# A gated cross-attention layer: PV and denominators in three bursts per 16 slots instead of four

## The chip, the cores and the metric

The kernel runs on one core of one Trainium2 chip. The metric is the time of one execution on the device in microseconds (us), the median of three runs. Profiles are of one execution each, and all times in them are counted from its first instruction.

## What is computed

Cross-attention with a tanh gate, and behind it a linear layer (called FFN in the code) with a gate of its own. Batch 8, 512 channels in 16 heads of 32, 1024 targets and 1024 sources, float32.

```python
q = einsum('oc,bct->bot', Wq, layernorm(x)) + bq      # k, v alike from ctx
dot = einsum('bhdt,bhds->bhts', q, k) / sqrt(32)
dot = mask * dot - (1.0 - mask) * 1e6
amap = softmax(dot, axis=-1) * mask
x = x + tanh(g_xattn) * einsum('bhts,bhds->bhdt', amap, v)
d1 = fp8(layernorm(x) * scale) / scale                # d2 alike from W2
x = x + tanh(g_ffn) * (d1 @ d2)
```

## The kernel before

A first part, up to some 580 us, projects q, k and v batch by batch and leaves them in DRAM. The second part is the attention. It works on **quads**: four heads of one batch, so 32 quads, `n` from 0 to 31. Each quad is a period of `NSLOT` = 64 **slots** `k`; two further periods drain the pipeline. All engines run through the same slots in program order and meet at semaphores, with no scheduler: what stands in which slot is written out by hand in the functions `slot` and `period` of each engine.

In a slot TensorE does two matmuls of 128x512: `scores` (line 833), whose result is keys by queries for the softmax of quad n, and `scores_for_max` (line 848), the same products the other way round, some of quad n and, from slot 19 (`XLEAD`) on, of quad n+1, from which VectorE takes the row maxima (`maximum`, line 1034, a reduction of 128x512). ScalarE takes the exponential of a score tile (`exp`, line 733) into `probs`, a ring of four chunks of four slots. The score tiles rotate through three PSUM banks, `s_bank`; the maxima tiles through three others, `x_bank`, in which `F_JOBS` also places four extra tenants: the turned maxima (`max1`, `max0`) and the FFN's two halves. So matmul k waits for what was done with the tile three places back:

```python
if counted(NSLOT * n + k - NB3 + 1):
    pe.wait_ge(exp_done, NSLOT * n + k - NB3 + 1)
```

Every four slots a chunk `c` of exponentials is complete. `times_v` (PV, line 863) multiplies it with V: four matmuls, one per head, each on 32 columns of the array, so they run side by side. Every eight slots GpSimd adds the two chunks of a **pair** `r` (`add_pair`, line 478, four additions of 128x512), and `denominators` (line 874) sums it over the keys with four such matmuls on `ones`. I call a set of four matmuls a group, and what stands between two slots' matmuls a burst. Chunk c must be consumed before chunk c+4 is written, pair r before pair r+2; exponentials of pair r+2's first slot wait for all of pair r's additions.

After 32 slots one half (`th`) of the queries is done. ScalarE copies output and denominators out (`copy_o`, `copy_den`), SyncE moves the denominators to 16 values a partition (`move_den`), VectorE inverts them (`invert`, lines 1059 and 1062), SyncE stores them to `inv_scr` (`move_inv`, line 594) and loads them spread over the heads' channels as `inv_b` (`spread_inv`, line 600). GpSimd's `weigh` (line 487) multiplies the copied output with `inv_b`, and `add_residual` (line 493) adds x. Then come the second layernorm and the rounding to fp8, in 15 numbered steps: VectorE's in the tables `NORM_AT` and `NORM_AT_2` (2 and 3 are `bn_stats`, line 1070), ScalarE's in `scale_rstd` and `normalize`, GpSimd's `pow`; then a DMA transpose, the FFN two quads later (`ffn`, line 889, eight matmuls for each half in two slots), `add_ffn` (line 1086) and the store. The next maxima go VectorE's `negate_max`, TensorE's `turn_max` (line 881), ScalarE's `copy_max`, SyncE's `set_max` (line 618) into two rows of `q_st`, which `scores` need from slots 0 and 32 on.

SyncE's issues stand in the fixed order of its `period`; each waits for its own data, and so holds up those behind it. `load_tm` (line 608) waits for the landing of the `inv_b` spread just ahead of it.

## Time and profile before

| | |
|---|---|
| median of three runs | 2563.50 us (2563.49 to 2564.08) |
| the profiled execution | 2563.17 us, of which 2561.4 from its first instruction to its last |
| TensorE, matmuls | 2481.3 us busy, 97% |
| VectorE | 1981.2 us, 77% |
| GpSimd | 1655.9 us, 65% |
| ScalarE | 1391.6 us, 54% |
| granted TensorE clock, mean | 0.990 |
| the attention loop | from some 580 us to the end |

A row of the table by stage has, for each stretch, the busy time of PE, PEld, DVE, ACT and POOL in this order. PE is TensorE, PEld its weight loads, DVE VectorE, ACT ScalarE, POOL GpSimd, SP SyncE (SPq its issues). A line such as "x4" in a timeline stands for four instructions of a kind merged into one row, with the time from the first one's start to the last one's end. A burst of four float32 matmuls shows eight records.

### The profile page before, as it was taken

To read this page: it belongs to the slowest core of one execution; us is meant where nothing else is said; L and a number is where in the kernel's file an instruction comes from. 1 tells how busy PE (TensorE), PEld (TensorE's weight loads), DVE (VectorE), ACT (ScalarE), POOL (GpSimd) and SP (SyncE) were. 2 spreads that over 40 slices of the span, in tenths; PEclk is the share of its full clock that TensorE was granted. 3 is DMA by queue.
4 is the path that set the end of the run, shared out by engine and by line. 5 is a ranking of instruction groups with operands and counts; after the bars stand their busy time and mean duration, and the time that the engine had idled before them with its cause. 6 is when DMAs were issued, how large, how long until landed. Compare 5 with 4: busy or idle time off the path is not lost.

```text
span 2561.4 us, 40583 instructions
## 1 busy us (share of the span) xinstructions
PE 2481.3 (97%) x13169; PEld 1380.6 (54%) x13169; DVE 1981.2 (77%) x3250; ACT 1391.6 (54%) x2606; POOL 1655.9 (65%) x1265
## 2 busy tenths in 40 slices
PE   5999999999999999999999999999999999999995
PEld 4888888874444444444444444444444444444441
DVE  5766666687788888888888888888888888888862
ACT  2333333315666666666666666666666666666562
POOL 1333333426777777777777777777777777777774
PEclk8999999999999999999999999999999999999997
DMA  6666666663444444444443444444444444444411
GB/s 208 239 237 238 239 237 238 238 195 94 95 98 101 102 97 95 90 94 96 92 90 90 90 90 95 93 93 96 100 101 98 101 101 94 93 94 91 97 31 50
DMA packets 242040, 314.49 MB, mean 123 GB/s; under 512 B 75032, under 2 KB 142680, under 8 KB 241856
## 3 DMA queue, kind: packets, MB, share of 16 engines
q1 hardware_dynamic: 229712, 274.20, 42.4%
q10 hardware_dynamic: 12144, 38.02, 4.2%
q8 instruction: 93, 1.52, 0.3%
q14 instruction: 91, 0.75, 0.1%
HBM read 200.09 MB, written 102.11 MB: 118 GB/s over the span
## 4 chain that ended last, share of the span: by engine, by line
PE 86%; DVE 6%; issue 3%; DMA 1%; POOL 1%; ACT 0%; SPq 0%; DVEq 0%; POOLq 0%; ACTq 0%
PE bank L818 20%; PE bank L833 19%; PE bank L863 18%; PE bank L848 16%; PE bank L874 8%; PE bank L889 5%; DVE part_max L1034 4%; POOL pair_sum L478 1%; PE bank L881 1%; DVE y L102 1%; DMA q_st<-qx_scr 0%; DVE isnan L101 0%; DMA v_scr<-stage 0%; POOL y L487 0%; DVE row_max L1043 0%
## 5 line engine op out<-in xcount | busy, mean ns | idle before, releaser
L478 POOL TENSOR_TENSOR pair_sum<-probs 128x512 f32<-128x512 f32 x1024 | 1284.9, 1287 | 425.2 <-ACT probs L733 425.2
L1034 DVE TENSOR_REDUCE part_max<-bank 128x1 f32<-128x512 f32 x2048 | 1282.1, 682 | 336.5 <-PE bank L848 329.1
L733 ACT ACTIVATE probs<-bank 128x512 f32<-128x512 f32 x2048 | 1071.1, 603 | 651.6 <-PE bank L833 648.0
L833 PE MATMUL bank<-q_st,k_st 100*128 100x512 f32 x2048 | 875.3, 429 | 5.1 <-ACT probs L733 5.0
L848 PE MATMUL bank<-k_st,q_st 98*128 98x512 f32 x2048 | 813.1, 397 | 7.6 <-DVE part_max L1034 5.5
L833 PEld LDWEIGHTS bank<-q_st,k_st 100*128 100x128 f32 x2048 | 386.5, 189 | 512.3 <-issue 264.9
L863 PE MATMUL bank<-probs,v_t 128*32 128x512 f32 x4096 | 546.3, 605 | 0.0
L848 PEld LDWEIGHTS bank<-k_st,q_st 98*128 98x128 f32 x2048 | 388.1, 190 | 112.9 <-DVE part_max L1034 9.9
L469 POOL TENSOR_TENSOR stage_lo<-stage,stage_hi 128x512 fp32r<-128x512 f32 x128 | 188.9, 1498 | 133.9 <-ACT stage_hi L697 133.0
L874 PE MATMUL bank<-pair_sum,ones 128*32 128x512 f32 x2048 | 267.4, 594 | 2.8 <-POOL pair_sum L478 2.8
L697 ACT ACTIVATE stage_hi<-stage 128x512 fp32r<-128x512 f32 x128 | 79.8, 632 | 200.6 <-DVE stage L948 140.0
L863 PEld LDWEIGHTS bank<-probs,v_t 128*32 128x32 f32 x4096 | 80.6, 108 | 144.0 <-ACT probs L733 75.5
L889 PE MATMUL bank<-w2q,y_t 128*128 128x512 bf16 x512 | 135.2, 390 | 23.1 <-DMA y_t<-y 22.7
L874 PEld LDWEIGHTS bank<-pair_sum,ones 128*32 128x32 f32 x2048 | 66.5, 110 | 156.3 <-issue 152.0
L457 POOL TENSOR_TENSOR rstd<-ve,neg_half 128x4 f32<-128x4 f32 x8 | 14.7, 1832 | 209.8 <-DVE ve L979 209.8
L818 PE MATMUL bank<-c_hi,w_hi_k 128*128 128x512 f32 x256 | 100.5, 393 | 13.8 <-DVE c_lo L931 13.8
L714 ACT ACTIVATE stage<-stage,sm_now 128x512 f32<-128x512 f32 x64 | 44.6, 720 | 120.9 <-DVE stage L944 120.9
L818 PE MATMUL bank<-w_hi_v,c_hi 128*128 128x512 f32 x256 | 100.2, 391 | 0.0
L818 PE MATMUL bank<-w_hi_v,c_lo 128*128 128x512 f32 x256 | 100.1, 391 | 0.0
L818 PE MATMUL bank<-c_hi,w_lo_k 128*128 128x512 f32 x256 | 100.1, 391 | 0.0
L818 PE MATMUL bank<-w_lo_v,c_hi 128*128 128x512 f32 x256 | 100.1, 391 | 0.0
L818 PE MATMUL bank<-c_lo,w_hi_k 128*128 128x512 f32 x256 | 100.1, 391 | 0.0
(95 smaller groups left out, 1966.0 us busy)
## 6 DMA issues: line engine op xcount, KB each, us to landing
k_st<-k_scr SPq DMA_DIRECT2D x96, 512.0 KB
q_st<-q_scr SPq DMA_DIRECT2D x192, 256.0 KB
c_raw<-in_ctx_dram ACTq DMA_DIRECT2D x32, 512.0 KB, 7.0
x_raw<-in_x_dram ACTq DMA_DIRECT2D x32, 512.0 KB, 6.3
k_scr<-stage_hi SPq DMA_DIRECT2D x64, 256.0 KB, 2.5
k_scr<-stage_lo SPq DMA_DIRECT2D x64, 256.0 KB, 2.7
v_scr<-stage SPq DMA_DIRECT2D x64, 256.0 KB, 2.9
q_scr<-stage_hi SPq DMA_DIRECT2D x64, 256.0 KB, 2.1
```

Of the source, the lines that this page charges most:

```text
L469: nc.gpsimd.tensor_tensor(stage_lo[:, e % STG], stage[:, g % STG], stage_hi[:, e % STG].bitcast(F32), ALU.subtract).then_inc(qk_lo, 1)
L478: nc.gpsimd.tensor_tensor(pair_sum[:, r % 2, h], probs[:, a, h], probs[:, a + 1, h], ALU.add).then_inc(pair_done, 1)
L697: nc.scalar.activation(stage_hi[:, e % STG], stage[:, g % STG], ACT.Copy).then_inc(qk_hi, 1)
L714: nc.scalar.activation(stage[:, g % STG], stage[:, g % STG], ACT.Copy, scale=sm_now[:, j:j + 1]).then_inc(v_masked, 1)
L733: nc.scalar.activation(probs[:, c % PR, h, :], s_bank_of(n, k)[:, :], ACT.Exp).then_inc(exp_done, 1)
L818: last = nc.tensor.matmul(acc, a, m, start=(cb == 0 and n == 0), stop=(cb == CB - 1 and n == 2))
L833: nc.tensor.matmul(s_bank_of(n, k)[:, :], k_st[p][0:KS, h, j * P:(j + 1) * P], q_st[p][0:KS, th, h, :], start=True, stop=True).then_inc(sc ...
L848: nc.tensor.matmul(x_bank_of(n, "tile", k)[:, :], q_st[p][0:KX, th, h, tc * P:(tc + 1) * P], k_st[p][0:KX, h, sh * HALF:(sh + 1) * HALF], ...
L863: last = nc.tensor.matmul(o_bank[D * h:D * (h + 1), :], v_t[p][:, j, D * h:D * (h + 1)], probs[:, c % PR, h, :], start=(j == 0), stop=(j = ...
L874: last = nc.tensor.matmul(d_bank[D * h:D * (h + 1), :], ones[:, :], pair_sum[:, r % 2, h, :], start=(i == 0), stop=(i == 3))
L889: last = nc.tensor.matmul(x_bank_of(n, f"ffn{half}", k)[:, :], y8_t[:, kc, :], w2q[:, kc, half * HALF:(half + 1) * HALF], start=(kc == 0), ...
L1034: nc.vector.tensor_reduce(part_max[:, th, sh, at:at + 1], x_bank_of(n, "tile", k)[:, :], AX, ALU.max).then_inc(max_done, 2)
```

## The change

The groups keep their number and shapes and get other slots. Written for 16 slots `16i` to `16i+15`: before, a burst stood behind slots 3, 7, 11 and 15, one PV group in each, and one denominator group more in those behind 3 and 11. After, bursts of two groups stand behind slots 5, 10 and 15: denominators and PV, denominators and PV, PV and PV. The side work on the other engines gets other slots, and `weigh` with `add_residual` stand behind GpSimd's pair 2 instead of pair 3.

```diff
-            F_JOBS = {23: "max1", 34: "ffn0", 50: "ffn1", 55: "max0"}
+            F_JOBS = {22: "max1", 40: "ffn0", 56: "ffn1", 54: "max0"}
@@ GpSimd, period
-                            if r == 3 and real(n - 1):
+                            if r == 2 and real(n - 1):
                                 weigh(n - 1)
                                 add_residual(n - 1, 1 - p)
@@ ScalarE, period
-                            if k == 3 and real(n - 1):
+                            if k == 5 and real(n - 1):
                                 copy_o(n - 1, 1)
-                            if k == 23 and real(n):
-                                copy_max(n, n, 1, 23)
-                            if k == 35 and real(n):
+                            if k == 22 and real(n):
+                                copy_max(n, n, 1, 22)
+                            if k == 37 and real(n):
                                 copy_o(n, 0)
-                            if k == 44 and real(n):
+                            if k == 45 and real(n):
                                 copy_den(n, 0)
-                            if k == 50 and real(n - 1):
+                            if k == 55 and real(n - 1):
                                 scale_rstd(n - 1)
-                            if k == 51 and real(n - 1):
+                            if k == 55 and real(n - 1):
                                 normalize(n - 1, 1 - p)
-                            if k == 55 and real(n + 1):
-                                copy_max(n, n + 1, 0, 55)
+                            if k == 54 and real(n + 1):
+                                copy_max(n, n + 1, 0, 54)
@@ TensorE, slot
-                        if k == 23 and real(n):
+                        if k == 22 and real(n):
                             turn_max(n, k, n, 1)
-                        if k == 55 and real(n + 1):
+                        if k == 54 and real(n + 1):
                             turn_max(n, k, n + 1, 0)
-                        for half, at_ in ((0, 34), (1, 50)):
+                        for half, at_ in ((0, 40), (1, 56)):
-                        if k % 4 == 3:
-                            if k >= 7 and real(n):
-                                times_v(n, p, (k - 7) // 4)
-                            if k < 7 and real(n - 1):
+                        i, at_ = k // 16, k % 16
+                        if at_ == 5:
+                            if i > 0 and real(n):
+                                denominators(n, 2 * i - 2)
+                                times_v(n, p, 4 * i - 1)
+                            if i == 0 and real(n - 1):
+                                denominators(n - 1, 6)
                                 times_v(n - 1, 1 - p, 15)
-                        if k % 8 == 3:
-                            if k >= 19 and real(n):
-                                denominators(n, (k - 19) // 8)
-                            if k < 19 and real(n - 1):
-                                denominators(n - 1, 6 + k // 8)
+                        if at_ == 10:
+                            if i > 0 and real(n):
+                                denominators(n, 2 * i - 1)
+                            if i == 0 and real(n - 1):
+                                denominators(n - 1, 7)
+                            if real(n):
+                                times_v(n, p, 4 * i)
+                        if at_ == 15 and real(n):
+                            times_v(n, p, 4 * i + 1)
+                            times_v(n, p, 4 * i + 2)
@@ VectorE, slot
-                    NORM_AT = {43: (2, 3), 44: (4,), 45: (5,), 59: (9, 10)}
-                    NORM_AT_2 = {3: (11,), 11: (12,), 19: (13, 14)}
+                    NORM_AT = {39: (2, 3,), 40: (4,), 44: (5,), 58: (9,), 61: (10,)}
+                    NORM_AT_2 = {3: (11,), 7: (12,), 14: (13,), 19: (14,)}
-                        if k == 19 and real(n):
+                        if k == 20 and real(n):
                             negate_max(n, 1)
-                        if k == 35 and real(n - 2):
-                            add_ffn(n, n - 2, p, 0, 34)
-                        if k == 51 and real(n - 2):
-                            add_ffn(n, n - 2, p, 1, 50)
+                        if k == 41 and real(n - 2):
+                            add_ffn(n, n - 2, p, 0, 40)
+                        if k == 58 and real(n - 2):
+                            add_ffn(n, n - 2, p, 1, 56)
-                        if k == 55 and real(n):
+                        if k == 54 and real(n):
                             invert(n, 0)
```

`invert(n - 1, 1)` stays at slot 23, `negate_max(n + 1, 0)` at 51, `copy_den(n - 1, 1)` at 12. SyncE's order of issues is the same. The line numbers after the change are 10 higher from VectorE's part on.

TensorE where the first half of the FFN stands, before: slot 34, the first four of its matmuls, slot 35, the other four, and the burst right behind them.

```order
L833 MATMUL bank<-q_st,k_st 128x512
L848 MATMUL bank<-k_st,q_st 128x512
L889 MATMUL bank<-w2q,y_t 128x512 x4
L833 MATMUL bank<-q_st,k_st 128x512
L848 MATMUL bank<-k_st,q_st 128x512
L889 MATMUL bank<-w2q,y_t 128x512 x4
L863 MATMUL bank<-probs,v_t 32x512 x4
L874 MATMUL bank<-pair_sum,ones 32x512 x4
```

The same place of the changed kernel, slots 40 to 42 and the burst behind 42.

```order
L889 MATMUL bank<-w2q,y_t 128x512 x4
L833 MATMUL bank<-q_st,k_st 128x512
L848 MATMUL bank<-k_st,q_st 128x512
L889 MATMUL bank<-w2q,y_t 128x512 x4
L833 MATMUL bank<-q_st,k_st 128x512
L848 MATMUL bank<-k_st,q_st 128x512
L874 MATMUL bank<-pair_sum,ones 32x512 x4
L863 MATMUL bank<-probs,v_t 32x512 x4
```

The second part of the half now has a slot behind it, and the burst begins with the denominators, here those of pair 3.

GpSimd, one quad of the middle, before: pair additions (28 from pair 5 of one quad to pair 3 of the next), the two long steps, pair 4, and the `pow`.

```order
L478 TENSOR_TENSOR pair_sum<-probs 128x512 x28
L487 TENSOR_TENSOR y<-o_raw,inv_b 128x1024
L493 TENSOR_TENSOR res<-res,y 128x1024
L478 TENSOR_TENSOR pair_sum<-probs 128x512 x4
L504 TENSOR_TENSOR rs<-ve,neg_half 128x1
```

And in the changed kernel:

```order
L478 TENSOR_TENSOR pair_sum<-probs 128x512 x24
L487 TENSOR_TENSOR y<-o_raw,inv_b 128x1024
L493 TENSOR_TENSOR res<-res,y 128x1024
L478 TENSOR_TENSOR pair_sum<-probs 128x512 x8
L504 TENSOR_TENSOR rs<-ve,neg_half 128x1
```

The four additions of pair 3 moved from in front of the two long steps to behind them.

VectorE in the changed kernel, from the inversion of the previous quad (slot 23) to slot 44: the reductions are those of the maxima tiles.

```order
L1069 RECIPROCAL inv_c<-den_c 128x16
L1072 SCALAR_TENSOR_TENSOR inv_c<-inv_c,g,tm_c 128x16
L1044 TENSOR_REDUCE part_max<-bank 128x1 x16
L1080 BN_STATS st<-res 128x6 x2
L1044 TENSOR_REDUCE part_max<-bank 128x1
L1082 BN_AGGR mv<-st 128x2
L1044 TENSOR_REDUCE part_max<-bank 128x1
L1096 SCALAR_TENSOR_TENSOR res<-bank,g,res 128x512
L1044 TENSOR_REDUCE part_max<-bank 128x1 x3
L1086 TENSOR_SCALAR ve<-mv 128x1
```

The two `bn_stats` now stand behind the tile of slot 39, the second of a run; before, they stood behind that of slot 43, the last ahead of a burst.

## Rows read from the trace of the kernel before

**Rows 1.** The page's span; one stretch: its length, busy us of five engines, clock, DMA, GB/s

```profile
span 2561.4 us, 40583 instructions
...
1500.00:2000.00 500.00, 497.38 (x2785) 240.51 (x2784) 411.21 (x711) 308.33 (x602) 372.29 (x288) 1.00 0.43 96
```

**Rows 2.** The list of waits of the whole run: total us, times, longest us

```profile
ACT o_raw L739 <- POOL y L487: 69.1, 31, 3.4
...
PE bank L848 <- DVE part_max L1034: 5.5, 5, 4.2
```

**Rows 3.** TensorE's timeline, 1500.9 to 1506.5: start us, us, engine, line, names

```profile
1500.87 0.39 PE L848 MATMUL bank<-k_st,q_st 98*128 98x512 f32 x1
...
1502.53 0.40 PE L848 MATMUL bank<-k_st,q_st 98*128 98x512 f32 x1
...
1503.94 0.40 PE L848 MATMUL bank<-k_st,q_st 98*128 98x512 f32 x1
...
1506.47 0.40 PE L848 MATMUL bank<-k_st,q_st 98*128 98x512 f32 x1
```

**Rows 4.** Timeline of all engines in the fourth slot of two runs

```profile
1496.04 1.29 DVE L1034 TENSOR_REDUCE part_max<-bank 128x1 f32<-128x512 f32 x2 [0.58 <-PE bank L848]
...
1496.79 0.19 PEld L848 LDWEIGHTS bank<-k_st,q_st 98*128 98x128 f32 x1
1496.94 0.40 PE L848 MATMUL bank<-k_st,q_st 98*128 98x512 f32 x1
...
1503.84 0.19 PEld L848 LDWEIGHTS bank<-k_st,q_st 98*128 98x128 f32 x1 [0.18 <-issue]
```

**Rows 5.** Timelines of VectorE and of ScalarE, 1502.8 to 1530.2

```profile
1503.03 2.48 DVE L1034 TENSOR_REDUCE part_max<-bank 128x1 f32<-128x512 f32 x4 [0.58 <-PE bank L848]
...
1507.00 2.48 DVE L1034 TENSOR_REDUCE part_max<-bank 128x1 f32<-128x512 f32 x4
...
1509.67 0.37 DVE L1062 SCALAR_TENSOR_TENSOR inv_c<-inv_c,g,tm_c 128x16 f32<-128x16 f32 x1
...
1528.78 1.41 DVE L1070 BATCH_NORM_STATS2 st<-res 128x6 f32<-128x512 f32 x2
...
1502.81 2.07 ACT L733 ACTIVATE probs<-bank 128x512 f32<-128x512 f32 x4 [0.51 <-PE bank L833]
```

**Rows 6.** TensorE's timeline around a turn and the FFN's two halves

```profile
1508.42 0.30 PE L881 MATMUL bank<-ident_r,neg_max 128*128 128x128 f32 x1
...
1517.91 0.39 PE L848 MATMUL bank<-k_st,q_st 98*128 98x512 f32 x1
...
1519.41 0.39 PE L848 MATMUL bank<-k_st,q_st 98*128 98x512 f32 x1
...
1520.61 1.06 PE L863 MATMUL bank<-probs,v_t 128*32 128x512 f32 x8
```

**Rows 7.** SyncE's timeline, 1510.4 to 1517.6

```profile
1510.46 0.71 SPq L618 DMA_DIRECT2D q_st<-max_rows  x1
1511.50 0.55 SPq L600 DMA_DIRECT2D inv_b<-inv_scr  x1
1516.50 1.06 SPq L608 DMA_DIRECT2D tm_c<-tm_scr  x2
```

**Rows 8.** GpSimd's timeline, 1519.9 to 1529.7

```profile
1519.88 2.37 POOL L487 TENSOR_TENSOR y<-o_raw,inv_b 128x1024 f32<-128x1024 f32 x1
...
1524.68 5.01 POOL L478 TENSOR_TENSOR pair_sum<-probs 128x512 f32<-128x512 f32 x4
```

**Rows 9.** DMA issues by line: KB each, median us to landing

```profile
out_dram<-res SPq DMA_DIRECT2D x32, 512.0 KB, 2.6
...
inv_scr<-inv_c SPq DMA_DIRECT2D x64, 8.0 KB, 1.4
```

**Rows 10.** SyncE's timeline in another quad, 1147.3 to 1153.0

```profile
1147.26 0.54 SPq L600 DMA_DIRECT2D inv_b<-inv_scr  x1
1151.91 1.06 SPq L608 DMA_DIRECT2D tm_c<-tm_scr  x2
```

More of the change, by code:

```diff
@@ L722, in batch @@
                             if not more and g == G - 4:
-                                copy_max(-1, 0, 0, 55)
+                                copy_max(-1, 0, 0, 54)
                     def exp(n, k):
```

## The prediction

> **What bounds the kernel now.** I read the page's span first, 2561.4 us, and then the table by stage: in a stretch of the attention loop TensorE is busy 497.38 of 500 us, at the full clock [rows 1]. So in that loop a microsecond taken from TensorE's stream shortens the run unless another engine takes its place. The list of waits says how near the others are: over the whole run TensorE waited 5.5 us for VectorE's row maxima, and ScalarE, not TensorE, waited 69.1 us for GpSimd's `y` [rows 2]. Then I read TensorE's timeline over one burst of each kind, and timelines of the other four engines for the slack.
>
> I write m(k) for the start of slot k's second matmul (the maxima one, line 848). Two slots apart without anything between them it is 0.467 us per slot (1503.94 less 1502.53 is 1.41 for three).
>
> **The saving in bursts.** A burst of one group takes m(k+1) to 1.66 us after m(k) (1500.87 to 1502.53), a burst of two groups to 2.53 us (1503.94 to 1506.47) [rows 3]. Less the plain slot that is 1.19 and 2.06 us. Before, 16 slots hold two of each, 6.50 us; after, three of two groups, 6.18 us. The work is the same six groups of four matmuls, and one entry and exit of about 0.32 us is gone. Per quad (64 slots) 4 x 0.32 = 1.28 us are saved. Groups in another order (denominators first, or two PV groups) have no row; between 1.74 us (no entry at all) and 2.38 us (two whole single bursts) I take 2.06, as the weight loads and columns are the same.
>
> **First loss: VectorE's lag with longer runs of slots.** A slot's maxima tile goes into one of three banks, so m(k+3) waits until the reduction of tile k has ended. The reduction starts 0.50 us after its matmul (1503.03 against 1502.53); four of them take 2.48 us, one 0.68, so the next starts every 0.60 us, slower than the 0.467 us of a slot [rows 3, 5]. In the fourth slot of a run the weight load already comes late: it starts at 1496.79, 0.07 us after the first reduction's end (1496.04 + 0.68), instead of with the matmul before it; its own matmul at 1496.94 still is on time, and in another run one started 0.10 us after such a load (1503.84, 1503.94) [rows 3, 4]. So m(i+3) cannot come before 0.50 + 0.60 i + 0.68 + 0.06 + 0.10 = 1.34 + 0.60 i us after the run's first. Runs of four slots: 1.34 against 1.40, no stall, as the trace has it. After, the runs are 6, 5 and 5 slots. Fifth slot: 1.94 against 1.87, a stall of 0.07. Sixth: 2.54 against 1.94 + 0.47, another 0.13, so 0.20 in a run of six. Per quad four runs of six lose 0.80. Of the eight runs of five, those with a `turn_max` (slots 22 and 54) lose nothing, since the turn spaces the slots out; five plain ones lose 0.35. In slots 38 to 42 the two halves of the FFN make the room (their slots take 1.50 and 1.20 + 0.13 us [rows 6]: natural length 3.77 us), but two `bn_stats`, 1.41 us, now stand after tile 39, and slot 42 needs tile 40: reduction from 3.03 us, end 3.71, m(42) at 3.87: 0.10 lost. Sum 1.25 us. VectorE's other steps stand behind the third tile of a run or further, or behind a tile that only the next run needs; the burst of 2.06 us covers them, as it does for the longest (1.2 us), with about 0.2 us to spare. Without that cover each costs what it sticks out. ScalarE's exponentials come every 0.49 us (2.07 less 0.60, over three) [rows 5], only 0.02 slower than a slot, and never gate six.
>
> **Second loss: GpSimd's two long steps ahead of pair 3.** `weigh` and `add_residual` move from behind the fourth pair addition to behind the third. `weigh` waits for `inv_b`, whose chain starts with `invert` behind tile 23 and is not moved. From m(23): 0.50 + 0.68 for the reduction, then 0.56 until the inversion's end (1509.67 + 0.37 less 1509.48), so 1.74 us. From there the way through two DMAs to the landing is 6.46 us: 1510.04 to 1516.50, where SyncE's next issue had waited for it [rows 5, 7]. Its longest part, from the issue of the second DMA to that point, is 5.00 us here and 4.65 us in the quad at 1147 [rows 7, 10], so 6.1 to 6.5 us in all. `weigh` and `add_residual` take 4.80 us (1519.88 to 1524.68), the four additions of pair 3 then 5.01 us [rows 8], handovers 0.10. So pair 3 is summed 1.74 + 6.46 + 4.80 + 5.01 + 0.10 = 18.11 us after m(23). TensorE wants it at slot 42, first thing in the burst (`denominators(n, 3)`). Its own way there: three slots 1.40, burst 2.53, slots 27 to 31 1.94, burst 2.53, slots 32 to 37 2.53, burst 2.53, slots 38 to 42 3.87, and 0.24 to the weight load: 17.57. It waits 0.54 us. Behind it stand that burst and every later slot. Before, pair 3 was added as soon as its exponentials were there and `weigh` began 3.4 us after the landing; that cover is spent. Exponential 40 also waits for pair 3, but its bank is wanted only after the burst.
>
> The Trainium skill (page "DMA: Bandwidth & Descriptors", section "Anatomy of one DMA — SWDGE (gpsimd) path") gives about 2.0 us plus bytes over 436 GB/s for one DMA, and so 2.6 us, an estimate, for the 256 KB of `inv_b`. The trace has 5.00 us from its issue to the next instruction that waits for it (1511.50 to 1516.50) [rows 7]. By the page the wait at slot 42 would vanish and the sum would end at 2564.
>
> **The other edits.** `turn_max` at slots 22 and 54: the transposed maxima are ready well over a microsecond earlier, behind a burst. FFN halves at 40 and 56, ScalarE's copies and normalize: each has a burst or two slots of slack; the price is nothing, up to 0.1 us per quad either way, since a turn or an FFN half now meets a slot instead of a burst. If `normalize` had no burst behind it, its 1.2 us would stop slot 59.
>
> **Sum.** Per quad -1.28 + 1.25 + 0.54 = +0.51 us. Thirty quads (1 to 30) have both losses: +15.3. Quad 0 has no `weigh`: 0. In the last quad the slots are shorter, so the wait for pair 3 is longer while the maxima losses end at slot 18, and in the tail `add_ffn` comes in front of one step of the last chain: about +1.5 together. The profiled execution took 2563.2 us (2561.4 between its first and last instruction), 0.3 below the median of the runs. 2563.5 + 16.8 is 2580.
>
> **The rivals.**
> - Pair 3 is in time (the way to slot 42 longer, or `inv_b` sooner, by over 0.54 us; a store of 512 KB lands in 2.6 us [rows 9]). Then the burst saving and VectorE's lag cancel: -1.28 + 1.25, 2564, no change. Against it: even the shorter 6.1 us leave 0.2 us of wait.
> - VectorE's lag doesn't stall (the weight load may begin before the reduction ends, or matmuls need less than 0.10 us behind it). TensorE then reaches slot 42 0.37 us earlier and waits 0.91: -1.28 + 0.91, 30 times, and 1.5: 2554, faster. For it: no such stall has a row in this trace. Against it: the weight load is seen held back to the reduction's end in the fourth slot. It decides once the five- and six-slot stalls are under half of what I say.
> - Neither loss comes: -1.28 x 31, 2524, faster. This is the change doing what bursts alone promise.
> - SyncE's queue. `store` now waits for the second `add_ffn` behind slot 58 instead of 51, and `set_max(n+1, 0)` stands behind it; slot 0 of the next quad needs that. The add ends 1.85 us after m(58); `store` and `move_inv` are issued first, at most 0.71 us each, so `set_max` is issued at 3.3 at most and lands 1.4 to 2.6 us later [rows 7, 9], by 5.9, against slot 0 at 2.53 + 1.94 + 2.19 = 6.66. Should it land like `inv_b`, after 5.0 us, slot 0 waits 1.6 us in every quad: 2628.
>
> **How the numbers follow.** Chances: as forecast 0.68; pair 3 in time 0.13; VectorE without stall 0.08; neither 0.05; SyncE's queue or another wait of that size 0.06. The likeliest gives 2580, its own range 2568 to 2592 (0.4 us per quad either way: the landing varies by 0.35, and a third of the VectorE stalls is as much). The whole range, taking in the case of no change and most of the faster one down to 2556, ends at 2596 above. Under 0.2%, 5.1 us, a measurement of this kernel can't tell a difference. Slower: 0.68 + 0.06 = 0.74, less a little for a forecast that shrinks, 0.72; within 0.2%: 0.15; faster 0.13.
>
> **What would show it.** In the profile after: m to m over every burst 2.53 us; in runs of five and six slots the fifth and sixth distance between line-848 matmuls over 0.467 by 0.07 and 0.13, with PEld's waits on `part_max` in the list; at the burst behind slot 42 a wait of about 0.5 us for `pair_sum` in every quad, with `y` (line 487) starting right at `inv_b`'s landing, some 8.6 us after the start of the turn (line 881) instead of 11.5 [rows 6, 8]; ScalarE's longest wait moves from `o_raw` to exponential 40. The forecast is wrong if line 874 never waits for `pair_sum`, if the burst costs more than 2.1 us, or if scores of slot 0 wait for `max_rows`.

## The result and the profile after

The changed kernel takes 2783.6 us, the median of four runs (2780.1 to 2789.4), against 2563.8 us for the kernel before on the same chip: ratio 1.086 (95% interval 1.084 to 1.087), 220 us more. The forecast had the direction and missed the size by far: 2580 us, range 2556 to 2596.

The page of the changed kernel: span, section 1, and the start of section 4, the chain that ended last.

```profile
span 2784.9 us, 40583 instructions
...
PE 2576.4 (93%) x13169; PEld 1392.7 (50%) x13169; DVE 2061.1 (74%) x3250; ACT 1391.5 (50%) x2606; POOL 1702.1 (61%) x1265
...
PE 56%; DMA 24%; POOL 5%; SPq 5%; DVE 4%; issue 4%; ACT 1%; DVEq 0%; POOLq 0%; ACTq 0%
PE bank L818 18%; DMA q_st<-qx_scr 18%; PE bank L848 11%; PE bank L833 10%; PE bank L863 8%; PE bank L874 6%; POOL pair_sum L478 4%; DMA inv_scr<-inv_c 3%; DMA inv_b<-inv_scr 3%; PE bank L889 2%; DVE part_max L1044 2%; SPq L570 2%; SPq L577 2%; POOL y L487 1%; DVE res L1096 1%
```

TensorE is busy 95 us longer with the same instructions, so it ran slower for a part of the time; the rest of the 223 us of span is idle. And 18% of the chain is a DMA that no step of the prediction named: `q_st<-qx_scr`, the last of those loads of the next quad's K and Q for which slot 19 waits.

The list of waits of the changed kernel (total us, times, longest us):

```profile
POOL pair_sum L478 <- PE bank L874: 282.6, 95, 8.7
...
PEld bank L848 <- DVE part_max L1044: 198.7, 602, 5.0
...
POOL y L487 <- DMA inv_b<-inv_scr: 191.2, 32, 13.5
...
ACT probs L733 <- POOL pair_sum L478: 98.7, 31, 4.9
PE bank L848 <- DMA q_st<-qx_scr: 97.1, 29, 4.5
...
PE bank L874 <- POOL pair_sum L478: 17.3, 18, 3.3
```

The waits for `part_max` and at L874, and `y` starting on the landing of `inv_b`, were forecast. The fifth line was not, and is the largest wait of TensorE's matmuls. None of the prediction's three signs of being wrong shows: L874 does wait, a double burst costs no more than 2.1 us, and no `scores` wait for `max_rows`. Where it comes from is on SyncE. First its timeline in the changed kernel at the end of a quad, then the same place before the change:

```profile
1453.36 0.36 SPq L627 DMA_DIRECT2D out_dram<-res  x1
1453.76 0.43 SPq L594 DMA_DIRECT2D inv_scr<-inv_c  x1
1454.23 0.74 SPq L618 DMA_DIRECT2D q_st<-max_rows  x1
1456.22 0.55 SPq L600 DMA_DIRECT2D inv_b<-inv_scr  x1
1456.87 1.37 SPq L570 DMA_DIRECT2D k_st<-k_scr  x3
...
1462.18 0.29 SPq L579 DMA_DIRECT2D q_st<-qx_scr  x1
```

```profile
1538.45 0.36 SPq L627 DMA_DIRECT2D out_dram<-res  x1
1542.29 0.34 SPq L594 DMA_DIRECT2D inv_scr<-inv_c  x1
...
1543.72 0.55 SPq L600 DMA_DIRECT2D inv_b<-inv_scr  x1
1547.74 1.29 SPq L570 DMA_DIRECT2D k_st<-k_scr  x3
```

Before, the store went out 4 us ahead of `inv_scr`, and the 256 KB of `inv_b` 4.0 us ahead of the K and Q loads. After, the store waits for `add_ffn` behind slot 58, everything behind it goes out in one lump, and `inv_b` is 0.65 us ahead of the loads. TensorE's timeline at slot 19, whose maxima matmul is the first to use the new K and Q:

```profile
1474.22 0.39 PE L833 MATMUL bank<-q_st,k_st 100*128 100x512 f32 x1
1478.82 0.80 PE L848 MATMUL bank<-k_st,q_st 98*128 98x512 f32 x1 [4.21 <-DMA q_st<-qx_scr]
1479.41 0.63 PE L833 MATMUL bank<-q_st,k_st 100*128 100x512 f32 x1
```

It stands 4.2 us, and the matmuls behind it take 0.63 us where those of [rows 3] take 0.40. The table by stage, around this wait (columns as in [rows 1]):

```profile
1458.10:1474.20 16.10, 16.10 (x90) 7.96 (x87) 14.88 (x22) 10.11 (x20) 13.42 (x11) 1.00 1.01 193
1474.20:1478.90 4.70, 0.49 (x3) 0.08 (x1) 1.24 (x3) 1.20 (x3) 0.61 (x1) 0.88 0.77 147
1478.90:1486.00 7.10, 7.10 (x27) 2.99 (x27) 3.36 (x8) 1.94 (x5) 2.58 (x3) 0.60 0.31 70
1486.00:1526.80 40.80, 40.15 (x226) 18.69 (x224) 32.42 (x57) 24.16 (x48) 30.21 (x23) 1.00 0.11 35
```

While the loads run (first row) the DMA engines are full, 1.01; the kernel before has 0.99 there (1548 to 1564 us). After the wait the granted clock is 0.60 over 7.1 us, most of that time at the lower level of 1.2 GHz, and then full again.

Where each quad's time goes I worked out from all records of `scores` in quads 4 to 29: mean us from one slot's `scores` to the next one's, the burst behind the slot included, and of that the time at 1.2 GHz. The columns e1, e5 and e8 are experiments further down, and "best" is the last one, e11.

```
slots                    after   e1      e5      e8      best
32 to 37 (run of six)    5.07    5.07    5.06    5.07    5.07
6 to 10 (run of five)    4.47    4.46    4.47    4.47    4.47
11 to 15                 5.04    5.05    5.05    5.03    5.03
19                       4.24    0.47    0.47    0.48    0.48
20, 21 (burst)           4.78    3.08    3.08    3.07    3.08
22 (turn)                0.90    3.34    0.63    0.63    0.63
23 to 26 (burst)         4.31    6.20    4.40    4.40    4.40
42 (burst, pair 3)       3.29    2.76    3.82    2.79    2.79
57                       2.09    2.15    2.02    2.18    1.34
all 64                  68.15   66.56   62.98   62.10   61.26
of that at 1.2 GHz       5.78    4.99    0.13    0       0
```

The kernel before takes 60.74 us for the same 64 slots, none of it at 1.2 GHz; there a slot with a double burst is 2.42, one with a single burst 1.55, the slot behind either 0.57 and a plain one 0.47. "after" less "best" is 6.89 us a quad: slots 19 to 26 5.6, slot 42 0.5, slot 57 0.75.

The forecast stalls themselves are there. TensorE's timeline at the end of a run of six slots, and at the burst behind slot 42:

```profile
1628.24 0.40 PE L848 MATMUL bank<-k_st,q_st 98*128 98x512 f32 x1
...
1628.71 0.48 PE L848 MATMUL bank<-k_st,q_st 98*128 98x512 f32 x1
...
1629.29 0.50 PE L848 MATMUL bank<-k_st,q_st 98*128 98x512 f32 x1
...
1636.78 1.07 PE L874 MATMUL bank<-pair_sum,ones 128*32 128x512 f32 x8 [0.61 <-POOL pair_sum L478]
```

### The profile page after: what moved, and what is told of

Its sections match the earlier page's. It is cut to its first block, busy times and chain, and to the rows that moved or that the text cites. A ratio compares the mean times of both kernels' runs of the same rounds, so it can differ in the third digit from the quotient of the medians.

```text
span 2784.9 us, 40583 instructions
## 1 busy us (share of the span) xinstructions
PE 2576.4 (93%) x13169; PEld 1392.7 (50%) x13169; DVE 2061.1 (74%) x3250; ACT 1391.5 (50%) x2606; POOL 1702.1 (61%) x1265
## 4 chain that ended last, share of the span: by engine, by line
PE 56%; DMA 24%; POOL 5%; SPq 5%; DVE 4%; issue 4%; ACT 1%; DVEq 0%; POOLq 0%; ACTq 0%
PE bank L818 18%; DMA q_st<-qx_scr 18%; PE bank L848 11%; PE bank L833 10%; PE bank L863 8%; PE bank L874 6%; POOL pair_sum L478 4%; DMA inv_scr<-inv_c 3%; DMA inv_b<-inv_scr 3%; PE bank L889 2%; DVE part_max L1044 2%; SPq L570 2%; SPq L577 2%; POOL y L487 1%; DVE res L1096 1%
## 5 line engine op out<-in xcount | busy, mean ns | idle before, releaser
L1044 DVE TENSOR_REDUCE part_max<-bank 128x1 f32<-128x512 f32 x2048 | 1298.9, 682 | 490.8 <-PE bank L848 488.4
L478 POOL TENSOR_TENSOR pair_sum<-probs 128x512 f32<-128x512 f32 x1024 | 1330.6, 1333 | 481.8 <-PE bank L874 282.6
L733 ACT ACTIVATE probs<-bank 128x512 f32<-128x512 f32 x2048 | 1085.5, 606 | 851.6 <-PE bank L833 744.9
L848 PE MATMUL bank<-k_st,q_st 98*128 98x512 f32 x2048 | 890.5, 435 | 122.0 <-DMA q_st<-qx_scr 97.1
L833 PE MATMUL bank<-q_st,k_st 100*128 100x512 f32 x2048 | 890.0, 436 | 2.1 <-ACT probs L733 1.9
L848 PEld LDWEIGHTS bank<-k_st,q_st 98*128 98x128 f32 x2048 | 397.3, 194 | 372.3 <-DVE part_max L1044 198.7
L863 PE MATMUL bank<-probs,v_t 128*32 128x512 f32 x4096 | 531.3, 614 | 0.0
L874 PE MATMUL bank<-pair_sum,ones 128*32 128x512 f32 x2048 | 298.0, 656 | 17.6 <-POOL pair_sum L478 17.3
L863 PEld LDWEIGHTS bank<-probs,v_t 128*32 128x32 f32 x4096 | 123.8, 113 | 280.4 <-issue 222.1
L487 POOL TENSOR_TENSOR y<-o_raw,inv_b 128x1024 f32<-128x1024 f32 x32 | 76.5, 2390 | 191.2 <-DMA inv_b<-inv_scr 191.2
```

The source lines that it names most:

```text
L478: nc.gpsimd.tensor_tensor(pair_sum[:, r % 2, h], probs[:, a, h], probs[:, a + 1, h], ALU.add).then_inc(pair_done, 1)
L487: nc.gpsimd.tensor_tensor(y[:, :], o_raw[:, :, :].rearrange("p a t -> p (a t)"), inv_b[:, :, :].rearrange("p a t -> p (a t)"), ALU.mult).t ...
L733: nc.scalar.activation(probs[:, c % PR, h, :], s_bank_of(n, k)[:, :], ACT.Exp).then_inc(exp_done, 1)
L833: nc.tensor.matmul(s_bank_of(n, k)[:, :], k_st[p][0:KS, h, j * P:(j + 1) * P], q_st[p][0:KS, th, h, :], start=True, stop=True).then_inc(sc ...
L848: nc.tensor.matmul(x_bank_of(n, "tile", k)[:, :], q_st[p][0:KX, th, h, tc * P:(tc + 1) * P], k_st[p][0:KX, h, sh * HALF:(sh + 1) * HALF], ...
L863: last = nc.tensor.matmul(o_bank[D * h:D * (h + 1), :], v_t[p][:, j, D * h:D * (h + 1)], probs[:, c % PR, h, :], start=(j == 0), stop=(j = ...
```

## The experiments

### Round 1: the queue, the burst table alone

**e1_store_last.** The changed kernel with SyncE's store moved behind the spread. Theory: the late store makes slot 19 wait. Rival: VectorE's side steps in the longer runs.

```diff
-                        if real(n - 2):
-                            store(n - 2, p)
                         if real(n):
                             move_inv(n, 0)
                         if real(n + 1):
                             set_max(n + 1, 0, 1 - p)
                         if real(n):
                             spread_inv(n, 0)
+                        if real(n - 2):
+                            store(n - 2, p)
```

> The changed kernel with one edit: SyncE issues the store of quad n-2 behind the spread of inv_b for (n, 0), at the end of its period, instead of in front of move_inv(n, 0). Theory Q (the queue): in the changed kernel that store waits for the FFN's second add behind slot 58, so the inv_b spread (256 KB, about 3.5 us of packets) is issued 1.9 us ahead of slot 0, right in front of the next quad's K and Q loads, and these land about 4 us later than slot 19 wants them; TensorE's idle time there also brings the granted clock to half for some 7 us. Then with this edit the spread is issued at least 4 us ahead of slot 0 again, the wait at slot 19 (now 3.6 us in the mean) is under 0.3 us, no stretch at half clock is left in the loop, and a quad takes 61 to 62 us: 2575 to 2600 us. Rival S (the slots): K and Q are late because of the new order of TensorE's bursts and the longer steps on VectorE and GpSimd; then the wait stays over 2 us and the time over 2720. Rival C (the clock gate alone, tripped by the waits at slot 42 and at the turns): the wait at slot 19 goes, but stretches at half clock stay, 2620 to 2700.

Measured: 2740.9 us, 1.069 (1.067 to 1.070). The wait at slot 19 is gone (0.47 in the table), which refutes the rival, and yet only 43 us came back, where 2575 to 2600 us were expected: behind slot 22 TensorE now waits for `neg_max` in nearly every quad. The timeline of all engines there, the list of waits, and the table by stage around it:

```profile
1591.69 3.72 POOL L478 TENSOR_TENSOR pair_sum<-probs 128x512 f32<-128x512 f32 x3 [2.29 <-PE bank L874]
1591.74 1.26 DVE L1053 TENSOR_TENSOR row_max<-part_max 128x16 f32<-128x16 f32 x1
...
1593.04 1.18 DVE L1058 TENSOR_SCALAR neg_max<-row_max 128x16 fp32r<-128x16 f32 x1
1594.26 1.19 DVE L1060 SCALAR_TENSOR_TENSOR neg_max<-row_max,neg_max 128x16 fp32r<-128x16 f32 x1
...
1595.50 0.47 PE L881 MATMUL bank<-ident_r,neg_max 128*128 128x128 f32 x1 [2.40 <-DVE neg_max L1060]
```

```profile
PE bank L881 <- DVE neg_max L1060: 69.5, 29, 2.4
```

```profile
1590.40:1595.50 5.10, 2.70 (x19) 0.72 (x19) 5.03 (x7) 1.17 (x3) 3.72 (x3) 0.98 0.31 65
1595.50:1600.50 5.00, 5.00 (x17) 3.08 (x21) 4.39 (x8) 2.66 (x5) 1.27 (x1) 0.50 0.02 3
```

Three steps on 16 columns take 1.2 us each. Where nothing meets them each takes 0.16 to 0.18 us, the shortest of the run; the median of the two `neg_max` steps is that too, 0.18 us, while `row_max` has a median of 0.87, as nearly all of them start beside an addition. They run beside three GpSimd additions of 1.24 us that begin at 1591.69, and each ends with one: 1593.00, 1594.22, 1595.45 against 1592.93, 1594.17, 1595.41. Behind the wait of 2.4 us the clock is 0.50, that is 1.2 GHz, for 5 us.

**e2_late_spread.** The kernel before, with SyncE held ahead of `spread_inv(n, 0)` until slot 62, so that `inv_b` goes out 0.9 us ahead of the loads. Nothing else is touched.

```diff
                         if real(n):
+                            sp.wait_ge(scores_ready, NSLOT * n + 62)
                             spread_inv(n, 0)
```

> The kernel before with one wait more: SyncE issues the inv_b spread of (n, 0) only when the scores of slot 61 are done, some 2 us ahead of slot 0, as in the changed kernel, instead of 5.1 us ahead. Nothing else differs; the value is not wanted before slot 28 of the next quad. Theory Q: K and Q land some 4 us later, a wait of 3 to 4 us at slot 19 appears in every quad with half clock behind it, a quad takes 66 to 68 us, 2700 to 2780 us in all. Rival S: no wait at slot 19, within 0.3% of 2564. A weaker form of Q (the spread matters only together with the store of 512 KB, which is issued 5 us ahead of slot 0 in the changed kernel): a wait of 1 to 2 us, 2600 to 2650.

Measured: 2662.6 us, 1.039 (1.032 to 1.045). The list of waits:

```profile
PE bank L849 <- DMA q_st<-qx_scr: 65.7, 28, 4.6
```

Slot 19 takes 5.93 us instead of 2.42, 2.9 us per quad fall at the lower clock, the quad takes 64.42 us instead of 60.74. The first K load goes out 1.1 us ahead of slot 0, exactly as in the kernel before, so the loads do not start later; they land later. The place of `inv_b` in the queue alone makes the wait in a kernel that had none. At 2663 us the loss is smaller than theory Q had it (2700 to 2780).

**e3_bursts_alone.** The kernel before with only the new burst table (the TensorE part of the diff from `i, at_ = k // 16, k % 16` on) and ScalarE's copies at 5, 37 and 45, where the groups end; turn, FFN, VectorE, GpSimd and SyncE as before.

```diff
-                            if k == 3 and real(n - 1):
+                            if k == 5 and real(n - 1):
                                 copy_o(n - 1, 1)
-                            if k == 35 and real(n):
+                            if k == 37 and real(n):
                                 copy_o(n, 0)
-                            if k == 44 and real(n):
+                            if k == 45 and real(n):
                                 copy_den(n, 0)
```

> The kernel before with TensorE's new bursts (three of two groups per 16 slots) and ScalarE's copies of outputs and denominators behind the groups they need (slots 5, 37, 45); turns, FFN, weigh, norm steps and invert stay where they were. By the sum of the prediction: bursts -1.28 us per quad; VectorE's lag +0.07 in the fifth and +0.13 in the sixth slot of a run, but turns and FFN halves (slots 23, 34, 50, 55) now stand inside runs and give room, so +0.8 to +1.1; pair 3 is not moved, no wait at slot 42. So -0.2 to -0.5 us per quad and 2548 to 2560 us, if no wait for K and Q appears at slot 19. Rival: VectorE's side work at slots 11, 35, 43, 51, which now stands early in a run, stalls TensorE by more than the bursts save: 2565 to 2600.

Measured: 2767.3 us, 1.080 (1.078 to 1.082). Here the side steps stand early in a run and no burst covers them: slots 15, 47 and 53 take 3.1 to 3.8 us, slot 63 5.85. The timeline of three engines at slot 63:

```profile
1644.05 1.65 DVE L94 TENSOR_SCALAR big<-big 128x1024 f32<-128x1024 f32 x1
...
1645.61 2.47 DVE L1042 TENSOR_REDUCE part_max<-bank 128x1 f32<-128x512 f32 x4
...
1646.35 0.49 PE L848 MATMUL bank<-k_st,q_st 98*128 98x512 f32 x1 [2.09 <-DVE part_max L1042]
```

The burst behind it runs partly at the lower clock. The rival was right about the side steps and, with 2565 to 2600 us, far too low about their price. So the new places of the side work are not the fault of the change as such: without them the new bursts cost nearly as much by another way.

**e4_store_last_weigh3.** e1 with `weigh` and `add_residual` back behind pair 3 (`r == 3`). 

> e1 and one edit more: weigh and add_residual stand behind GpSimd's pair 3 again. By the prediction's second loss pair 3 then is in time for slot 42: 0.5 us per quad less than e1, so 12 to 20 us faster than e1, with no wait for pair_sum at the burst behind slot 42. Rival: bn_stats at slot 39 now waits for the residual, holds up the maxima tile of slot 40 and gives the gain back: within 5 us of e1.

Measured: 2748.7 us, 1.072 (1.071 to 1.074), nothing gained over e1, where 12 to 20 us were expected. In e1 the wait for `pair_sum` at L874 is 6.5 us in the whole run: the 2.4 us at the turn had given GpSimd the time. The forecast wait can't be seen as long as a longer one stands ahead of it.

### Round 2: GpSimd beside VectorE

**e5_negate_early.** e1 with `negate_max(n, 1)` behind tile 19, ahead of the additions, and step 14 in its place.

```diff
-                    NORM_AT_2 = {3: (11,), 7: (12,), 14: (13,), 19: (14,)}
+                    NORM_AT_2 = {3: (11,), 7: (12,), 14: (13,), 20: (14,)}
-                        if k == 20 and real(n):
+                        if k == 19 and real(n):
                             negate_max(n, 1)
```

> e1 (the changed kernel with the store last in SyncE's period) and one edit more: VectorE's negate_max stands behind the tile of slot 19, as before the change, and norm step 14 behind slot 20. In e1 the turn behind slot 22 waits 2.5 us a quad for neg_max: negate_max, three short steps behind slot 20, falls together with GpSimd's pair 2, which starts as soon as the denominators behind slot 21 are done, and each step takes about 1.2 us instead of 0.17. Theory P (VectorE's steps on SBUF wait for GpSimd's running addition): at slot 19 GpSimd is idle, the three steps take 0.17 us each again, the turn's wait and the half-clock stretch behind it go: 4 to 5 us a quad less than e1, 61.5 to 63 us, 2590 to 2630 us. Rival C (the clock falls for another reason, such as the form of the new bursts): the wait goes but some 5 us a quad at half clock stay: 2660 to 2700.

Measured: 2636.6 us, 1.027 (1.025 to 1.029), 7 us above the range of theory P. Slot 22 falls from 3.34 to 0.63 us, the time at the lower clock from 5.0 to 0.1 us per quad. Now the wait for pair 3 is out in the open: slot 42 takes 3.82 us, and the list of waits has

```profile
PE bank L874 <- POOL pair_sum L478: 34.6, 31, 3.3
```

**e6_half_additions.** e1 with each pair addition on 256 of its 512 columns, 1.0 standing in the other half. It leaves out the sum for half the columns. Theory: VectorE's long steps wait for the running addition, so shorter additions shorten them.

```diff
-                            nc.gpsimd.tensor_tensor(pair_sum[:, r % 2, h], probs[:, a, h], probs[:, a + 1, h],
-                                                    ALU.add).then_inc(pair_done, 1)
+                            nc.gpsimd.tensor_tensor(pair_sum[:, r % 2, h, 0:HALF // 2], probs[:, a, h, 0:HALF // 2],
+                                                    probs[:, a + 1, h, 0:HALF // 2], ALU.add).then_inc(pair_done, 1)
```

> e1 with GpSimd's pair additions on 256 of 512 columns; it leaves out the sum over the other half of the columns, which holds ones, so the denominators there are wrong and the rest is unchanged. An addition then takes about 0.65 us instead of 1.25. Theory P: a VectorE step that meets GpSimd waits for at most the addition under way, so neg_max's two steps fall from 1.19 to about 0.6 us, y (L98) from 2.13 to about 1.5, isnan from 0.94 to 0.6 or less, the wait at the turn from 2.5 to about 0.7, and with it the half clock goes: 2600 to 2650. Rival D (these steps are long because the DMA traffic of K and Q slows VectorE's SBUF access, or by their own place): their durations stay at 1.1 us and over, and the time stays within 1% of e1.

Measured: 2579.0 us, 1.005 (1.003 to 1.007), faster than the 2600 to 2650 of theory P. The view of one tile, `neg_max`, in e1 and then in e6 (min/median/max in ns):

```profile
L1060 DVE SCALAR_TENSOR_TENSOR neg_max<-row_max,neg_max x56: 174/177/1186, 630.1 to 2460.9; 128x16 fp32r<-128x16 f32 x56
```

```profile
L1060 DVE TENSOR_SCALAR neg_max<-row_max x61: 174/176/679, 628.9 to 2464.8; 128x16 fp32r<-128x16 f32 x61
```

(The two edits shift the line numbers against each other, so L1060 is the second step there and the first here; both steps read 174 to 177 where nothing meets them.) The longest goes from 1.19 to 0.68 us as the addition's median goes from 1.28 to 0.73 us, and `y<-y,big` (line 98) from 2.13 to 1.77. How long these two wait is thus set by the addition's length. One step does not follow: `isnan` has a median of 0.94 in e1 and, in e6,

```profile
L101 DVE TENSOR_SCALAR isnan<-y x29: 411/982/998, 714.3 to 2429.2; 128x1024 bf16<-128x1024 bf16 x29
```

where 0.6 or less was expected; why it stays long no run shows. Slots 11 to 15 go from 5.05 to 4.68, slot 22 from 3.34 to 1.20, slot 57 to 1.34, and no time is left at 1.2 GHz.

**e7_before_negate21.** The kernel before with `negate_max(n, 1)` at slot 21 instead of 19. 

> The kernel before with one edit: negate_max for th = 1 stands behind the tile of slot 21 instead of 19; the turn stays behind slot 23. In the trace of before GpSimd's pair 2 begins at about slot 21. Theory P: the three steps of negate_max now meet those additions, take about 1.2 us each, the turn waits some 2 us in every quad, and the granted clock drops behind that wait as in e1: 2 to 4 us a quad, 2620 to 2690 us. Rival (the length of these steps comes from something else in the new order): they stay at 0.17 us, no wait, 2560 to 2570.

Measured: 2728.8 us, 1.066 (1.062 to 1.069), 65.64 us per quad, more than the 2620 to 2690 us expected: two slots' delay of three short steps costs 165 us. The list of waits:

```profile
PE bank L881 <- DVE neg_max L1050: 94.2, 31, 3.3
```

Slot 23 takes 5.44 us instead of 2.01, and 4.6 us per quad pass at the lower clock.

### Round 3: how much comes back

**e8_weigh3.** e5 with `r == 3`. 

> e5 and one edit more: weigh and add_residual behind GpSimd's pair 3 again, as before the change. In e5 TensorE waits 1.4 us a quad for pair 3 at the burst behind slot 42, the second loss of the prediction, larger than its 0.54. If that loss is what the move of the two steps costs, slot 42 takes 2.4 to 2.5 us instead of 3.8 and a quad 61.5 to 61.8: 2595 to 2605 us. Rival: pair 4 or the bn_stats of slot 39, which need the residual, become late instead, and the time stays over 2620.

Measured: 2612.6 us, 1.019 (1.017 to 1.020), above the 2595 to 2605 expected. Slot 42 goes from 3.82 to 2.79 us, not to 2.4 to 2.5: with nothing else in the way the order on GpSimd costs 1.03 us a quad.

**e9_invert56.** e8 with `invert(n, 0)` behind tile 56 instead of 54. 

> e8 and one edit more: invert(n, 0) behind the tile of slot 56 instead of 54. In e5 slot 57 takes 2.0 us against 1.34 with shorter GpSimd additions (e6), since the second step of invert meets GpSimd in the first slot of a run and tile 55 comes late. Two slots on, only the next run wants the tiles behind it: 0.6 us a quad less than e8, 2575 to 2590 us. Rival: the inversion now comes too late for SyncE, the spread of inv_b moves towards the K and Q loads, and the wait at slot 19 comes back: over 2620.

Measured: 2595.0 us, 1.012 (1.010 to 1.014). Slot 57 falls from 2.18 to 1.34, but the spread goes out later, now 3.2 us ahead of the loads, and the wait at slot 19 is back with 0.6 us a quad. Both expectations hold in part, and the time lies between the two.

**e10_negate_only.** The changed kernel with e5's edit alone, the store left early in the queue. 

> The changed kernel with e5's edit alone (negate_max behind slot 19, step 14 behind 20), the store where the change has it. In the changed kernel the wait for K and Q at slot 19 gave negate_max time, so the wait at the turn hardly shows; if the two causes hide each other in this way, mending the second alone brings little: 2760 to 2785 us, with the wait at slot 19 and the half clock unchanged. Rival (they add up): 2740 or less, as e5 gained 104 us over e1.

Measured: 2764.7 us, 1.078 (1.076 to 1.080), as expected. The same edit that gains 104 us behind e1 gains 19 us here: the wait at slot 19 stays (slot 19 takes 4.44 us), and behind it VectorE has caught up by itself.

**e11_spread_behind.** e9 with the spread issued behind the next quad's K and Q loads.

```diff
                         if n > 0 and real(n + 1):
                             stack_k(n + 1, 1 - p)
                             stack_q(n + 1, 1 - p)
+                        if real(n - 1):
+                            spread_inv(n - 1, 0)
...
-                        if real(n):
-                            spread_inv(n, 0)
```

> e9 and one edit more: SyncE issues the spread of inv_b for (n, 0) behind the next quad's K and Q loads instead of ahead of them; it is wanted only at weigh, more than 25 slots later. In e9 slot 19 waits 0.6 us again, with the spread 3.0 us ahead of the loads' first issue. Theory Q: that wait goes, a quad takes 61.1 to 61.3 us, 2574 to 2585 us. No version with the new bursts is then expected to beat the kernel before: the plain losses of VectorE's lag (1.15 us a quad) and of its steps that meet GpSimd (0.6 us in slots 11 to 15 alone) are larger than the 1.3 us that the bursts save. Rival: the wait at slot 19 comes from elsewhere (the later invert), and stays.

Measured: 2581.0 us, 1.006 (1.005 to 1.008), as theory Q had it, and the best that keeps the new bursts and computes the reference. Its table by stage and its list of waits:

```profile
1500.00:2000.00 500.00, 495.77 (x2748) 234.81 (x2764) 424.98 (x702) 304.98 (x597) 386.37 (x286) 1.00 0.46 96
```

```profile
PE bank L848 <- DVE part_max L1044: 11.4, 11, 4.6
PE bank L874 <- POOL pair_sum L478: 3.7, 1, 3.7
```

In quads 4 to 29 no long wait is left and the clock is full, and it is still 17 us behind the kernel before. No version beat the kernel before.

## Why the prediction missed

**The saving in bursts: right.** A slot with a double burst is 2.42 us, one with a single 1.55, and the slot behind each has 0.10 more; less a plain slot (0.47) the bursts cost 2.05 and 1.18, against 2.06 and 1.19 forecast. Per 16 slots 2 x (2.05 + 1.18) less 3 x 2.05 is 0.31 us, so 1.24 a quad are saved, against 1.28. In none of the kernels does a double burst that nothing delays cost more.

**"First loss", VectorE's lag: right, in mechanism and size.** A run of six takes 5.07 us against 4.87 without a stall (0.20 forecast, 0.20 measured), a plain run of five 4.47 against 4.40 (0.07 and 0.07). For slots 38 to 42 the table's slot 42 (2.79 in e8, against 2.42 for a double burst) does not show the lag by itself: a slot behind an FFN half is longer without any lag, since its maxima matmul starts 0.42 us after its `scores` instead of 0.24. In the prediction's own measure, from m(38) to m(43), the forecast was 3.87 + 2.53 = 6.40 us with 0.10 of stall in it; e6 has 6.40 and e11 6.48 (medians). With 4 x 0.20 and five times 0.07 the lag is 1.25 to 1.33 us a quad, against 1.25. The rival of a lag without stall is refuted.

**"Second loss", pair 3: right in the changed kernel, short where nothing longer hides it.** 0.54 us forecast; 0.5 in the changed kernel (3.29 less 2.79), and 1.03 in e5 (less e8). The traces say which term grew. In the changed kernel pair 3 is summed 18.30 us after m(23), against 18.11 in the forecast; in e5 it is 19.07 (medians). The inversion explains it: it ends 1.64 us after m(23) in the changed kernel and 2.69 in e5, against 1.74 in the forecast, because in e5 its last step meets an addition. The tile `inv_c` in e5:

```profile
L1072 DVE SCALAR_TENSOR_TENSOR inv_c<-inv_c,g,tm_c x59: 234/1299/1394, 631.7 to 2458.7; 128x16 f32<-128x16 f32 x59
```

The way from there to the landing is 6.39 us in e5, against 6.46 forecast. So the term that was short is the inversion, by the same cause as the second failed step below. The rival in which pair 3 is in time is refuted, and with it the 2.6 us for `inv_b`: the Trainium skill's figure (page "DMA: Bandwidth & Descriptors", section "Anatomy of one DMA — SWDGE (gpsimd) path") would have left no wait, and the wait came. From issue to last landing these loads take 4.8 us here (before, median). The section's heading gives the figure for GpSimd's path, and SyncE issues this load; whether that is the difference no run shows.

**"SyncE's queue": the step that failed.** The prediction looked at one thing behind the late store, `set_max`, found it in time, and gave waits of that kind 0.06. It did not follow the queue further, to the loads of the next quad. What stands ahead of them is a transfer of 256 KB that before had 4.0 us to itself and now has 0.65. e2 makes the wait in the kernel before with that one edit; e1 and e11 take it away, the one by an earlier spread, the other by a spread behind the loads; e9, at 3.2 us, has a part of it. From the records of issues and landings, medians in us over 25 quads:

```
                                 before   e1    e11     e9    e2    after
spread ahead of the first load    4.0     5.2  behind   3.2   0.9    0.65
first load ahead of slot 0        1.1     2.1   2.1     2.1   1.1    1.2
last landing slot 19 wants,
  after the first load's issue   15.6    15.7  15.8    18.6  19.1   21.3
```

The loads had little slack to lend: before, slot 19's maxima start 16.9 us after the first load's issue, without a wait; after, 21.3 us after it. In the changed kernel the held queue also costs the loads 0.8 us of their own start (1.2 us ahead of slot 0, where e1 has 2.1). The store is not the cause, as a rival would have it: in e1 its 512 KB go out 2.7 us ahead of the loads and they land on time. e2 makes 3.5 of the 5.7 us by which the landing moved; the other 2.2, in a queue where the store goes out 3.5 us ahead of the loads and the spread 0.3 us closer to them, no run took apart.

The DMA shares hint at why so small a transfer weighs so much. Two stretches of the kernel before in which the spread alone runs:

```profile
1512.50:1514.00 1.50, 1.50 (x14) 0.52 (x7) 0.47 (x1) 0.00 (x0) 0.01 (x1) 1.00 0.25 72
1514.00:1515.50 1.50, 1.50 (x8) 1.04 (x6) 1.09 (x2) 1.31 (x3) 0.57 (x1) 1.00 0.26 100
```

It keeps a quarter of the 16 engines' time busy, as four engines would, while the loads take 0.99 of it. If it does run on four, the loads' pieces on those four wait for all of it; that is argued from the shares, not shown. Together with what it does to the clock this is some 5.6 us a quad: slots 19 to 26, after less best.

**"VectorE's other steps ... with about 0.2 us to spare": the second step that failed.** I took their durations as fixed, though they change with what GpSimd does beside them: in the kernel before the last step of `invert` has a median of 0.38 us and a longest of 1.34, and takes 0.23 where nothing meets it (the shortest of e5); `row_max` has a median of 0.37 and a longest of 1.34. The view of the tile `y`, before and then after, shows two of them (min/median/max in ns):

```profile
L98 DVE TENSOR_TENSOR y<-y,big x30: 1211/1214/1433, 708.9 to 2470.3; 128x1024 bf16<-128x1024 f32 x30
L101 DVE TENSOR_SCALAR isnan<-y x30: 418/419/422, 716.4 to 2477.7; 128x1024 bf16<-128x1024 bf16 x30
```

```profile
L98 DVE TENSOR_TENSOR y<-y,big x26: 2120/2126/2149, 712.3 to 2415.3; 128x1024 bf16<-128x1024 f32 x26
L101 DVE TENSOR_SCALAR isnan<-y x26: 937/952/974, 718.6 to 2421.5; 128x1024 bf16<-128x1024 bf16 x26
```

The steps did not change; what runs beside them did. Before, the additions were released by ScalarE's exponentials, now by TensorE's denominators, which take two groups in one burst and let go of a pair at another time. The lists of waits, before and after (after, 282.6 us for L874 come ahead of it, the first line of the list above):

```profile
POOL pair_sum L478 <- ACT probs L733: 425.2, 194, 4.1
```

```profile
POOL pair_sum L478 <- ACT probs L733: 198.7, 82, 5.8
```

In slots 11 to 15, behind `y<-y,big` of slot 7, that costs 0.6 us a quad (5.04 against the 4.47 of slots 6 to 10; 4.68 in e6), at slot 57 0.75 (2.09 less 1.34), and at the turn, once the queue is mended, 2.7 (e1's slot 22 less e5's) and the clock behind it. e6 shows that the additions' length sets it, e7 that the place does.

**The clock: not in the sum at all.** The prediction priced each wait at its length. The waits of e1 (2.4 us), e7 (up to 3.3), e2 and the change (up to 4.6) brought with them 3 to 6 us a quad at 1.2 GHz, at which matmuls take up to twice their time; those of about 1 us in e5 next to none. Per quad the waits of e1 last 2.4 us and cost 4.5 (its slots 22 to 26 less e5's), those of e7 3.0 and 4.9, those of e2 2.3 and 3.7, those of the change 3.3 and 5.6: 1.6 to 1.9 times what they last.

**Causes that hide each other.** e4 against e8 (nothing, or 24 us) and e10 against e5 (19 or 104 us) are the same edits with and without a longer wait ahead. Undone one at a time in the changed kernel, either would have looked small.

**The account.** Best less before is 0.52 us a quad. Bursts -1.2, lag +1.3, steps beside additions in slots 11 to 15 +0.6 and in slots 22 to 26 +0.2; slots 54 to 58, with the turn and an FFN half in one run, -0.2, and slot 11's 0.1 over a double burst's 2.42 before is gone: +0.6, against 0.52. The last three terms are differences of the table that no run tested singly. With pair 3 (0.5), slot 57 (0.75) and slots 19 to 26 (5.6) it is the 7.4 us of the table (68.15 less 60.74); over the 29 quads that have the wait at slot 19 that is 215 of the 220 us. That e11 lands on 2581, near the forecast, is another sum and no support for it.

## What to carry to other kernels

When an issue in a queue is made to wait longer, follow the queue to its end, past the next consumer, and ask of every large transfer behind it what it will now share the DMA engines with and how much slack that one's reader has. A duration read where a neighbour engine is idle holds only there: before a step is moved, see what runs beside the new place, and price it with that. Price a wait of TensorE of 2 to 4 us at 1.6 to 1.9 times its length, as it was here, and remove suspects cumulatively, since the longest wait hides the others. Signs of being wrong that only watch the steps of one's own sum miss a loss outside it.

## What the runs showed of the hardware

- Some VectorE steps from SBUF to SBUF wait for a GpSimd addition of 128x512 that runs when they come: 0.17 to 1.19 us (16 columns, ending with the addition), 0.42 to 0.95 (`isnan`), 1.21 to 2.13 (`y<-y,big`). Others, with one SBUF input or none, don't: beside additions the reciprocal of 16 columns takes 0.24 us and `bn_stats` of 128x512 0.69 as ever, and the reductions of the maxima tiles, which read PSUM, 0.68. The Trainium skill (page "SBUF — State Buffer", section "SBUF: two separate sides") says that VectorE and GpSimd share a pair of SBUF ports as "an exclusive lock, not a bandwidth split", for steps in a 2-port mode or with two SBUF inputs, against a GpSimd step that reads SBUF. The trace agrees: in e1 each of the three steps ends within 0.07 us of an addition. L1058 there has one tensor input; whether it ran in a 2-port mode no row shows.
- The K and Q loads land up to 4.6 us late for slot 19 with the 256 KB spread issued 0.65 us (after) or 0.9 us (e2) ahead of them; at 3.2 us (e9) slot 19 still takes 1.07 us instead of 0.47, at 4.0 us (before) there is no wait. While they run together the DMA share is 1.01, with the spread alone 0.25 to 0.27. A store of 512 KB issued 2.7 us ahead (e1) did not delay them.
- The clock stayed near 2.4 GHz through waits of about 1 us once a quad (e5, 0.13 us a quad at the lower level), and stood at 1.2 GHz for 5.0 us a quad with waits of 2.4 us (e1).
